# ScalarE's row sums of a recommendation tower: read out into SBUF instead of a PSUM bank with a copy per tile

## What is computed

```
e = stack([tbl_f[ids[:, f]] for f in range(32)], axis=1)      # 1024 x 32 x 64
p, q = e[:, ROW], e[:, COL]                                    # all 496 pairs of fields
z = einsum('bne,hne,bnh->bn', p, kernel, q)                    # 1024 x 496
h = concatenate([z, dense_ctx], axis=1)                        # 1024 x 512
h = maximum(h @ W_top1 + b_top1, 0)                            # 512 x 512
h = maximum(h @ W_top2 + b_top2, 0)                            # 512 x 256
y = h @ W_top3                                                 # 256 x 1
```

## Time and profile before

| | us |
|---|---|
| median of 3 runs | 402.61 |
| lowest, highest | 401.84, 402.92 |
| the profiled execution, whole | 402.61 |
| its span in the profile | 400.8 |
| TensorE busy in the span | 371.6 (93%) |
| VectorE busy | 354.9 (89%) |
| ScalarE busy | 315.4 (79%) |
| GpSimd busy | 241.8 (60%) |

### The profile page before, as it was taken

The page is one execution under the profiler, slowest core; times in us unless marked ns, Lnnn a source line. Parts: engine busy times, 40 slices in busy tenths (PEclk is TensorE's granted clock), DMA queues, the critical chain, the costliest instruction groups (busy, mean ns, idle before and its releaser), DMA issues.

```text
span 400.8 us, 13206 instructions
## 1 busy us (share of the span) xinstructions
PE 371.6 (93%) x4464; PEld 277.7 (69%) x4464; DVE 354.9 (89%) x512; ACT 315.4 (79%) x2887; POOL 241.8 (60%) x260
## 2 busy tenths in 40 slices
PE   0468889899999999999999999999999999999987
PEld 0244657587777877678777877778777877778666
DVE  0249999899999999999999999999999999999971
ACT  1157696897969987898869987798869988798862
POOL 5677777766666666676676666666666666640000
PEclk9968999999999999999999999999999999999999
DMA  3566792111111111111111111111111111110000
GB/s 82 173 196 198 226 262 41 26 27 24 26 26 24 25 25 27 23 28 26 25 27 24 25 25 24 29 25 26 24 25 26 25 28 23 25 21 3 2 2 2
DMA packets 14563, 19.25 MB, mean 48 GB/s; under 512 B 7192, under 2 KB 7840, under 8 KB 14496
## 3 DMA queue, kind: packets, MB, share of 16 engines
q0 software_dynamic: 8192, 8.40, 11.2%
q1 hardware_dynamic: 6304, 10.00, 7.9%
HBM read 18.39 MB, written 0.00 MB: 46 GB/s over the span
## 4 chain that ended last, share of the span: by engine, by line
PE 84%; DVE 5%; POOL 4%; issue 3%; DMA 2%; ACT 1%; DVEq 0%
PE u_ps L570 28%; PE u_ps L577 26%; PE side_ps L591 14%; PE side_ps L625 7%; POOL emb L363 4%; PE side_ps L636 3%; PE u_ps L555 2%; DVE prod_s L502 2%; DVE prod_t L484 2%; DMA emb<-tbl,ids_sb 2%; ACT prod_s L404 1%; PE u_ps L657 1%; PE side_ps L649 1%; PE side_ps L617 1%; DVE emb_t L471 1%
## 5 line engine op out<-in xcount | busy, mean ns | idle before, releaser
L404 ACT ACTIVATE prod_s<-prod_s 128x64 f32<-128x64 f32 x1408 | 293.0, 372 | 77.1 <-DVE prod_s L502 76.6
L363 POOL DMA_INDIRECT emb<-tbl,ids_sb x256 | 241.6, 944 | 114.6 <-issue 35.4
L404 ACT ACTIVATION_READ_ACCUMULATOR prod_s<-prod_s 128x1 f32 x1408 | 277.2, 287 | 0.0
L484 DVE TENSOR_TENSOR prod_t<-u_ps,emb_t 128x1024 f32<-128x1024 f32 x128 | 155.7, 1217 | 8.0 <-PE u_ps L570 7.3
L502 DVE TENSOR_TENSOR prod_s<-u_ps,emb 128x512 f32<-128x512 f32 (+4 forms) x224 | 151.2, 721 | 11.1 <-PE u_ps L577 10.5
L570 PEld LDWEIGHTS u_ps<-emb_t,k_sb 64*128 64x128 f32 x2048 | 129.2, 190 | 36.8 <-DVE prod_s L502 12.8
L570 PE MATMUL u_ps<-emb_t,k_sb 64*128 64x128 f32 x2048 | 139.5, 279 | 3.3 <-DVE emb_t L471 1.5
L577 PE MATMUL u_ps<-k_sb,emb_t 64*128 64x512 f32 (+5 forms) x704 | 128.0, 483 | 3.7 <-DVE emb_t L471 2.1
L577 PEld LDWEIGHTS u_ps<-k_sb,emb_t 64*128 64x128 f32 x704 | 63.2, 192 | 26.9 <-issue 11.3
L591 PE MATMUL side_ps<-prod_t,pick_sb 128*32 128x256 f32 x1024 | 63.3, 382 | 0.0
L511 DVE TENSOR_REDUCE h<-prod_s 128x4 f32<-128x256 f32 x128 | 52.4, 409 | 0.0
(11 more groups left out here) (23 smaller groups left out, 38.3 us busy)
## 6 DMA issues: line engine op xcount, KB each, us to landing
k_sb<-k_pairs SPq DMA_DIRECT2D x9, 512.0 KB, 4.0
emb<-tbl,ids_sb POOLq DMA_INDIRECT x256, 2.5
k_sb<-k_pairs SPq DMA_DIRECT2D x6, 480.0 KB, 4.6
w_sb<-w SPq DMA_DIRECT2D x1, 1024.0 KB
w_sb<-w SPq DMA_DIRECT2D x1, 512.0 KB
k_sb<-k_pairs SPq DMA_DIRECT2D x1, 448.0 KB, 3.9
h<-dense SPq DMA_DIRECT2D x8, 8.0 KB
out<-y_row SPq DMA_DIRECT2D x8, 0.5 KB
```

What stands on the lines that cost most here:

```text
L363: nc.gpsimd.indirect_dma_start(emb[t % EMBS][:, f * EMBED:(f + 1) * EMBED], None, tables[f], bass.IndirectOffsetOnAxis(ap=ids_sb[:, t, f:f ...
L404: done = nc.scalar.activation(slot, slot, ACT.Copy, accum_out=acc_ps[:, t % 2, column:column + 1])
L484: done = nc.vector.tensor_tensor(prod_t[at % TRING][:].rearrange("p (h x) -> p h x", h=HALVES), u, low.unsqueeze(1).to_broadcast([P, HALVE ...
```

## The change

The sums that ScalarE reads out go straight into `h0[t]`, into the columns that the copy filled before. The copy `copy_acc` and its semaphore are gone, 8 instructions. The transposes wait for ScalarE's sums themselves (`summed_a`). The bank that held the sums is now used by the last tile's transposes alone, under a new name. Line numbers behind the removed lines are lower by 5 to 8 in the changed kernel.

```diff
-        acc_ps = ctx.enter_context(nc.psum_tensor("acc_ps", [P, 2, 2 * P], F32))
+        spread_bank = ctx.enter_context(nc.psum_tensor("spread_bank", [P, 4, P], F32))
...
-        acc_copied = sem("acc_copied")
...
-        spread_ps = acc_ps[:, (last + 1) % 2].rearrange("p (c b) -> p c b", c=S_CHUNKS)
+        spread_ps = spread_bank[:, :S_CHUNKS]
...
-                    done = nc.scalar.activation(slot, slot, ACT.Copy, accum_out=acc_ps[:, t % 2, column:column + 1])
+                    done = nc.scalar.activation(slot, slot, ACT.Copy, accum_out=h0[t][:, column:column + 1])
                 done.then_inc(summed_a, 1)
-
-            def copy_acc(t):
-                act.wait_ge(summed_a, (t + 1) * NS)
-                nc.scalar.activation(h0[t][:, :ON_ACT], acc_ps[:, t % 2, :ON_ACT], ACT.Copy).then_inc(acc_copied, 1)
...
-                    if t > 0 and n == 0:
-                        copy_acc(t - 1)
...
-            copy_acc(last)
             act.wait_ge(last_turned, 1)
...
             def spread_straight(t, to):
                 pe.wait_ge(summed_v, (t + 1) * NS)
-                pe.wait_ge(acc_copied, t + 1)
+                pe.wait_ge(summed_a, (t + 1) * NS)
```

## The result

The changed kernel takes 413.45 us (413.32 to 414.06), the kernel before 402.62 (401.84 to 402.92): a ratio of 1.0275, 95% interval 1.0257 to 1.0293. It is slower by 10.8 us. The profiled execution took 413.34 us with a span of 411.5, against 402.61 and 400.8.

A forecast was written before the change was run, and what follows sets the result against it. TensorE, busy 93% of the span, was taken to set the time. Six steady tiles 13.0, first tile 1.0, end 0.42 less 0.35 for the copy: 14.1 us on 402.61, forecast 416.7 us, range 402.0 to 419.

The forecast's parts named there:

- the likeliest case: Each ScalarE pair takes about 0.042 us longer with its sum read into SBUF; chance 0.50, own range 413 to 419 us.
- x: Extra time of a ScalarE pair (ACTIVATE and read of its sum) when the read writes SBUF, not PSUM; taken as 0.042 us.
- The missing copy, the wait: Eight copies removed: nothing inside a tile, 0.35 us gained at the end; the waits for `summed_a` instead cost nothing.
- Step (a): From ScalarE's idle time through 32 pairs to `copy_spread`: ScalarE 1.10 us later, room 1.02, TensorE 0.1 late.
- Step (b): After `copy_spread`, 56 pairs up to `hidden1`: ScalarE 3.20 us late, room 2.33, TensorE 0.87 late.
- Step (c): From `hidden1` past `hidden2` to `copy_logit`: ScalarE 2.77 us late, room 0.61, TensorE 2.16 late in all.
- The first tile: First tile with a network has 8.1 us of ScalarE idle, 1.9 more than the others; loss taken as 1.0 us.
- The ring: Ring of `prod_s` buffers between ScalarE's reads and VectorE's multiplies: does not bind, room 5.9 us.
- x = 0: Rival: the SBUF destination costs latency only, so only the end changes, 402.3 us; chance 0.30.
- the long hold: Rival: next ACTIVATE waits for the read's SBUF write, near 0.1 us more a pair, about 475 us; chance 0.05.

The follow-up runs named there:

- The probe: Kernel before plus 28 activations of 128x64 in ScalarE's idle start, seven forms of four; plain starts 0.146 us apart reading SBUF, 0.104 reading PSUM; no kernel time given.

## Why the prediction was right, and where it was off

It gave 416.7 us with the likeliest case at 413 to 419; measured were 413.45. The side and the mechanism were right, the sum was 14.1 us for 10.8. The time lies just inside the lower end of the likeliest case, because the delay of TensorE in a tile was put at 2.16 us and is 1.70.

- **x.** Forecast 0.042 us for a pair, measured 0.042. The number was right and its reason half wrong, so that it came out so exactly is in part luck. I took it that an ACTIVATE holds the engine by where it writes and carried this over to the read. The probe showed that a plain ACTIVATE goes by where it reads from, and that in the kernel's pairs the destination counts for the read alone. The copy of the earlier trace rows, which reads PSUM and yet holds the engine 0.09 us beyond its elements, was what led me off. The copy of 512 columns from PSUM, with nothing to wait for behind it, holds it only 0.05 in the changed kernel (220.99 to 221.46 for 0.427 us of elements). Why the old copy of 176 held it 0.04 longer stays open.
- **The missing copy, the wait.** Nothing inside a tile, as forecast. At the end, from the last block's first pair to TensorE's transposes, 2.61 us instead of 2.63: -0.02, where 0.42 - 0.35 = +0.07 was forecast. The first pair and the transposes' weight load before, and the same with the last read after:

```profile
388.58 0.26 ACT L404 ACTIVATE prod_s<-prod_s 128x64 f32<-128x64 f32 x1 [3.33 <-DVE prod_s L502]
...
391.21 0.20 PEld L617 LDWEIGHTS acc_ps<-id_sb,h 128*128 128x128 f32 x2 [2.01 <-issue]
```

```profile
399.32 0.26 ACT L403 ACTIVATE prod_s<-prod_s 128x64 f32<-128x64 f32 x1 [2.87 <-DVE prod_s L494]
...
401.63 0.19 ACT L403 ACTIVATION_READ_ACCUMULATOR prod_s<-prod_s 128x1 f32 x1
401.93 0.20 PEld L609 LDWEIGHTS spread_bank<-id_sb,h 128*128 128x128 f32 x2 [2.00 <-issue]
```

- **Step (a), the first matrix.** Forecast 0.1 us late. Measured 0: `copy_spread` ends at 221.56, TensorE comes at 221.85. The step's start came 1.11 us later, for a forecast of 1.10, but its end only 0.80: its row is 0.57 us, was 0.88.
- **Step (b), `hidden1`.** Its start came 3.15 us later (12.99 us behind the start of TensorE's first matrix, against 9.84), forecast 3.20. Most of that 0.05 is the copy of 512 columns, which holds ScalarE 0.477 us and not the 0.52 that the half-wrong rule gave. But its end came only 2.66 later, and TensorE was late by 0.30 instead of 0.87. This is the term that was mis-sized. The four activations last 1.10 us in the changed kernel, 1.59 in the earlier trace rows, because ScalarE's ends lagged before. In the earlier trace rows the read's own row grows from 0.15 us to 0.42 in the course of a run of pairs, some 0.0085 with each; in the changed kernel it stays between 0.18 and 0.23. I had these rows and took ends and starts as moving together. The slower pair gives part of its cost back by ending on time.
- **Step (c), `copy_logit`.** Forecast 2.77 us late at its end and TensorE 2.16; measured 2.35 and 1.70. This term too was mis-sized. 0.14 of the difference is the same lag (its row is 0.25 us, was 0.39). The rest came before its start (2.49 instead of 2.77), most of it from an idle time that I read too small: an idle time in the timeline counts from the end of the last read, and that end lagged too.

```profile
231.33 0.23 ACT L404 ACTIVATION_READ_ACCUMULATOR prod_s<-prod_s 128x1 f32 x1
```

  ScalarE was free 0.05 us behind the start of this read, so it had 1.66 us before 233.05 and not the 1.49 of the earlier trace rows.
- **The first tile, the sum.** 0.7 us for the forecast 1.0. Six tiles at 1.70, the first at 0.7 and the end at 0 make 10.9. Between the spans are 10.7; the changed kernel's trace is 0.13 us ahead at the first tile's first matrix (81.59 against 81.72), before ScalarE can hold anything up, so 10.8 are left to compare. Of the forecast's excess 6 x 0.46 = 2.8 us are in the steady tiles, 0.3 in the first and 0.1 at the end. ScalarE's idle time fell to 2.7 us a tile, not to some 1, for the same reason as in step (c).
- **The ring.** No row of the list has VectorE waiting for ScalarE. As forecast.
- **The rivals.** x = 0 and the long hold fell with the pair's 0.239 us. The page of the Trainium skill, Perfetto Trace Analysis (DVE / Act Engine Instruction), by which the next instruction may begin to fetch once its forerunner has executed, agrees with the probe for every plain ACTIVATE: its destination makes no difference to the next start. It does not hold for the read of a sum, which costs 0.042 us more into SBUF; the measurement decides. The note of the Trainium skill, ScalarE: Activation LUTs (Step-by-step), that ScalarE writes PSUM faster, agrees with the rows' ends in the probe: 0.21 against 0.24 us for the same 64 elements from SBUF.

## What to carry to other kernels

Where ScalarE makes many short sums, the memory that the sum is read out to is part of the price of each: 1408 times 0.042 us here, against one copy a tile of 0.24 us. Whether the kernel pays for it is decided at the few places where another engine waits for something that stands behind those sums in ScalarE's order, so look there for the room before you count the load. If such a place binds, moving the awaited step ahead of a block of sums can be worth as much as making the sums faster: on the one chip that ran both it took the cost from 0.46% to none that could be told. Where the engine is as full as on the first chip, 44.4 us in a tile of 45.4, that was not tried.

## What was not expected of the hardware

- A plain ACTIVATE of 64 elements follows its forerunner after 0.146 us if it reads SBUF and 0.104 if it reads PSUM, wherever it writes; behind an ACTIVATE that reads SBUF, the read of an accumulated sum holds 0.093 us into SBUF and 0.05 into PSUM. Such a pair takes 0.197 us into PSUM, 0.239 into SBUF. With a PSUM input it is shorter and irregular, 0.16 to 0.20 us with the sum in PSUM.
- In a run of pairs with their sums in PSUM the ends fall behind the starts, by some 0.0085 us a pair and up to about 0.5 us, until the engine waits for something. With their sums in SBUF they fall behind by no more than 0.04 us.
- In the lots of the experiments, on two chips, the kernel before took 57 and 64 us longer, with pauses of up to 1.2 us in the midst of a run on ScalarE and on TensorE; on the one of them that ran the changed kernel the change cost 0.46% instead of 2.75%.
